# Loading x for the first read from a second copy laid out for it, in pieces of one chunk over 128 partitions with 8 KB rows

## The reference

```
xn = layernorm(x)                                  # over the 2048 channels
qkv_in = rat_read(xn)    # 4 channels of each of 512 groups -> 3 x 512, normalised, gamma and beta
q, k, v -> rope -> causal attention, 16 heads of 32 -> attn_out
h = rat_write(xn, attn_out); m = rat_read(h) -> gate, up (2048 wide) -> silu(gate) * up
h = rat_write(h, m)
x = x + tanh(g_xattn) * h
x = x + tanh(g_ffn) * (layernorm(x) @ sign) * softplus(scale)
```

## Time and profile before

| | |
|---|---|
| time of the kernel before, median of 3 runs | 2212.17 us (2210.51 to 2214.36) |
| profiled execution, its own time | 2214.25 us |
| its span in the profile | 2212.4 us |
| PE busy | 1981.1 us (90%) |
| DVE / ACT / POOL busy | 1415.1 / 978.9 / 423.3 us |
| moved by DMA | 453.87 MB, 205 GB/s on average |

### The profile page before, as it was taken

One profiled execution on the slowest core, in us unless ns is written; L12 is line 12 of the kernel. 1 busy time (PEld: TensorE's weight loads), 2 busy tenths in 40 slices (PEclk: granted clock), 3 DMA queues, 4 the chain that ended last, 5 costly groups with the idle time before them and its releaser, 6 DMA issues.

```text
span 2212.4 us, 25095 instructions
## 1 busy us (share of the span) xinstructions
PE 1981.1 (90%) x9562; PEld 1378.9 (62%) x9562; DVE 1415.1 (64%) x1563; ACT 978.9 (44%) x1376; POOL 423.3 (19%) x325
## 2 busy tenths in 40 slices
PE   2789897999999996289989999999999999989997
PEld 0344456666566553157767777777777677766786
DVE  3677767677777755958657638758639658468100
ACT  3656652787788875044145233143341162431100
POOL 1000004676555550000000001110001000011111
PEclk9899997999999997699999999999999999999999
DMA  8848346686666743246666657777658677559675
GB/s 198 186 110 187 91 102 207 238 289 235 239 239 223 265 171 128 100 165 235 230 238 225 248 186 218 233 243 261 227 191 234 207 263 277 224 162 258 156 183 136
DMA packets 180924, 453.87 MB, mean 205 GB/s; under 512 B 64320, under 2 KB 64576, under 8 KB 165440
## 3 DMA queue, kind: packets, MB, share of 16 engines
q1 hardware_dynamic: 146160, 313.31, 42.3%
q0 software_dynamic: 32480, 128.46, 20.9%
q10 hardware_dynamic: 2160, 10.43, 1.3%
HBM read 304.80 MB, written 147.32 MB: 204 GB/s over the span
## 4 chain that ended last, share of the span: by engine, by line
PE 44%; DVE 7%; DMA 5%; ACT 4%; issue 2%; SPq 0%; POOL 0%; DVEq 0%; POOLq 0%; ACTq 0%
PE ps L1788 16%; PE ps L1598 8%; PE ps L1600 7%; PE ps L1599 7%; DMA sign_h<-sign_h_scratch 2%; DMA up<-up_s_scratch 2%; PE ps L1657 1%; PE ps L1666 1%; PE ps L1695 1%; ACT L1817 1%; PE ps L1618 1%; DVE Y L2111 1%; PE ps L1707 1%; DVE DL_attn L2018 0%; DVE E_attn L2023 0%
## 5 line engine op out<-in xcount | busy, mean ns | idle before, releaser
L1788 PE MATMUL ps<-XH,sign_h 128*128 128x512 f32 x768 | 308.9, 402 | 13.5 <-DMA sign_h<-sign_h_scratch 8.7
L1788 PE MATMUL ps<-XL,sign_h 128*128 128x512 f32 x768 | 302.9, 394 | 0.0
L1159 DVE TENSOR_REDUCE maxes<-ps 128x1 f32<-128x512 f32 (+3 forms) x384 | 207.8, 554 | 97.4 <-PE ps L972 75.0
L1598 PE MATMUL ps<-ZH,up 128*128 128x512 f32 x512 | 205.3, 401 | 15.5 <-DVE ZL L2136 8.9
L1599 PE MATMUL ps<-ZL,up 128*128 128x512 f32 x512 | 201.0, 392 | 0.0
L1600 PE MATMUL ps<-ZH,up 128*128 128x512 f32 x512 | 200.9, 392 | 0.0
L1086 ACT ACTIVATE probs<-ps 128x512 f32<-128x512 f32 (+3 forms) x384 | 167.5, 485 | 50.6 <-PE ps L999 29.9
L1788 PEld LDWEIGHTS ps<-XH,sign_h 128*128 128x128 f32 x768 | 146.0, 190 | 60.9 <-issue 13.0
L969 PE MATMUL ps<-turned_k,turned_q 96*128 96x512 f32 (+3 forms) x384 | 157.6, 424 | 12.0 <-DVE maxes L1159 10.0
L1015 PE MATMUL ps<-probs,v_ones 128*64 128x512 f32 (+3 forms) x768 | 167.3, 514 | 0.3 <-ACT probs L1086 0.3
L1788 PEld LDWEIGHTS ps<-XL,sign_h 128*128 128x128 f32 x768 | 146.3, 191 | 31.6 <-issue 1.9
(11 more groups left out here) (334 smaller groups left out, 4169.4 us busy)
## 6 DMA issues: line engine op xcount, KB each, us to landing
sign_h<-sign_h_scratch SPq DMA_DIRECT2D x256, 256.0 KB, 3.8
up<-up_s_scratch SPq DMA_DIRECT2D x58, 1024.0 KB, 6.4
proj<-proj_s_scratch SPq DMA_DIRECT2D x58, 640.0 KB, 4.1
X<-in_x POOLq DMA_DIRECT2D x16, 1024.0 KB, 15.4
xn_scratch<-X SPq DMA_DIRECT2D x16, 1024.0 KB, 14.2
sign_raw<-in_sign SPq DMA_DIRECT2D x32, 512.0 KB, 7.9
sign_h_scratch<-sign_high SPq DMA_DIRECT2D x32, 512.0 KB, 4.0
sign_l_scratch<-sign_low SPq DMA_DIRECT2D x32, 512.0 KB, 5.3
```

Source lines behind the costliest of these rows:

```text
L1159: eng.tensor_reduce(MAXES[:, e, q, k0 // T:k0 // T + 1], ps[:, MX[m % 2], 0:w], AX.X, ALU.max).then_inc(mx_read.sem, mx_read.unit)
L1598: eng.matmul(out_ap, lh, rh, start=start, stop=False, skip_group_check=True)
L1788: mm = eng.matmul(ps[:, sign_bank(m)], s[q][:, f], x[:, n], start=n + w == 0, stop=n == NF - 1 and w == len(operands) - 1, skip_group_chec ...
```

## The change

The program gets a further input, `x_read`, which holds the same values as `x` in another order: [4 tiles, 4 chunks, 128 partitions, 2048], laid out before launch exactly as X wants it. A transfer now carries one chunk a of a tile for all 128 partitions: 128 rows of 8 KB, which stand one behind the other in HBM. There are again four transfers of 1 MB for a tile, C = HC = 4, so the waits' values stay as they are. The stores of xn keep `rows_of_x` and their four blocks of 32 partitions.

```diff
+def piece_of_x(t, x_read, a, n):
+
+    return (t["X"][:, n % 2, a * C:(a + 1) * C], x_read[n, a])
...
                 eng.wait_ge(loaded.sem, loaded.at(k=len(loads)))
-                for c in range(C):
-                    eng.dma_start(*rows_of_x(t, io["x_c"], c, 0)).then_inc(t["x_in"][0].sem, t["x_in"][0].unit)
+                for a in range(HC):
+                    eng.dma_start(*piece_of_x(t, io["x_read"], a, 0)).then_inc(t["x_in"][0].sem, t["x_in"][0].unit)
...
                 eng.wait_ge(w_in.sem, w_in.at(0, 4))
-                for c in range(C):
-                    eng.dma_start(*rows_of_x(t, io["x_c"], c, 1)).then_inc(x_in[1].sem, x_in[1].unit)
+                for a in range(HC):
+                    eng.dma_start(*piece_of_x(t, io["x_read"], a, 1)).then_inc(x_in[1].sem, x_in[1].unit)
                 for n in range(2, NB):
                     half = n % 2
                     eng.wait_ge(xn_out[half].sem, xn_out[half].at(n // 2 - 1, C))
                     eng.wait_ge(rd.sem, rd.at(n - 2, 3 * HC))
-                    for c in range(C):
-                        eng.dma_start(*rows_of_x(t, io["x_c"], c, n)).then_inc(x_in[half].sem, x_in[half].unit)
+                    for a in range(HC):
+                        eng.dma_start(*piece_of_x(t, io["x_read"], a, n)).then_inc(x_in[half].sem, x_in[half].unit)
...
+    io["x_read"] = args["x_read"].rearrange("n a p (j t) -> n a p j t", j=C)
...
         "x": x.reshape(B * L, HC, P, C).transpose(3, 1, 2, 0).reshape(NF, P, B * L),
+        "x_read": x.reshape(NB, T, HC, C, P // C, C).transpose(0, 2, 5, 4, 3, 1).reshape(NB, HC, P, C * T),
```

More of the change, by code:

```diff
@@ L2237, in build @@
     io["xn"] = xn.rearrange("f p t -> p f t")
-    for name, rows in (("x_c", args["x"]), ("xn_c", xn)):
-        io[name] = [rows[c * HC:(c + 1) * HC].rearrange("a (j h) t -> h (a j) t", j=C) for c in range(C)]
+    io["xn_c"] = [xn[c * HC:(c + 1) * HC].rearrange("a (j h) t -> h (a j) t", j=C) for c in range(C)]
+    io["x_read"] = args["x_read"].rearrange("n a p (j t) -> n a p j t", j=C)
     for name, shape in (("up_s", [NM, P, 2, 2 * HC * P]), ("proj_s", [NM, P, 2, WALL]), ("wall_s", [P, HC, 2, WALL]),
```

## The result

Over 15 timed executions the changed kernel takes 2202.37 us at the median, the kernel before 2218.05 us over 15. The ratio is 0.9935, 95% interval 0.9922 to 0.9948: 14.4 us faster, between 11.5 and 17.3 (the two medians lie 15.7 apart, inside that). The first three runs of the kernel before, 2212.17 at the median, were at the low end of its scatter (2210.5 to 2224.6). The profiled execution took 2199.85 us, its span is 2198.0 against 2212.4.

The account below looks back on a forecast made before the run. The prediction took PE's waits for two loads of X, tiles 0 and 3, as the bound; 11.6 + 4.0 = 15.6 us off the 2212.17 us median gave 2196.6 us, range 2191 to 2203.

Parts of the forecast that it names:

- from the median of 2212.17 it is 2196.6: Whole kernel: the summed gain of 15.6 us, taken off the median of the runs shown, gives 2196.6 us.
- the rest keeps its lengths: After the read phase: attention begins 15 to 16 us earlier and everything else takes as long as before.
- The first wait: Program start: the whole core waits for the load of tile 0; 11.6 us less, PE starting at about 17.4.
- 3.15 us are issue, first bytes and the last confirmation: Load of tile 0: fixed 3.15 us of the old 24.45, kept beside 9.75 us of transfer in the new load.
- The other route, x_last: Load of tile 0: four existing 1 MB, 128-partition loads on POOL's queue took 12.7 us, so tile 0 would take about that.
- The second wait: Tile 3 in the read phase: PE's 2.45 us stall and 1.5 us of lower-clock matmuls both go, 4.0 us together.
- The covered loads: Tiles 1 and 2 in the read phase: their loads are hidden before and after, so they gain nothing.
- rival 5: Block phase: the added input moves scratch tensors and slows up and sign weight streams; 2218.6 us at 25% growth, chance 0.03.
- rival 3: Tile loads: HBM or the queue gives only 326 GB/s, gain 8.4 + 4.0 us, time 2199.8 us; chance 0.05.
- The prediction's 88 us for those waits: Block phase: waits for up and sign weights, 2% + 2% of the span on the chain, put at some 88 us.
- The sum: Whole kernel: 11.6 us at the start plus 4.0 us at tile 3 make 15.6 us.

Follow-up runs that it names:

- the tile 0 kernel: Changed kernel with only tile 0 loaded in the new form, tiles 1 to 3 as before; ratio 0.9963 to the kernel before.
- the tile 3 kernel: Changed kernel with only tile 3 loaded in the new form, the others as before; ratio 1.0001 to the kernel before, 0.9970 when timed again.
- the kernel with the added input: Changed kernel with only tiles 1 and 2 loaded in the new form, the new 16.8 MB input present; ratio 1.0004 to the kernel before.

## Why the prediction came out as it did

**The step that failed** is the base of the sum, "from the median of 2212.17 it is 2196.6", and with it "the rest keeps its lengths". Both take the time of what the change does not touch as fixed, and three runs as enough to know it. The runs showed in its place 2218.05 us at the median of 15, and 2214.7 to 2218.4 in four further sets. They also showed an attention part of 499.6 or 505.1 us and a block part of 1356.0 or 1348.2 us in one and the same kernel. The base was 5.9 us too low, and the predicted time 5.8. The profiled execution of the kernel before, 2214.25 us, had the short attention part. That the three runs had it as well would explain the low base, but is not shown. Beside this, one term of the gain was mis-sized, as follows.

**The first wait.** Predicted 11.6 us, PE's start at 17.4. Measured 10.9 in the first profile; over all profiles of the two kernels the start is 28.88 on average before (28.99, 28.77) and 17.76 after (18.13, 17.69, 17.46), 11.1 us. The mechanism, the released barrier with all engines at once, is as described. The term that was mis-sized is "3.15 us are issue, first bytes and the last confirmation". It came from the old load, as the rest beyond 21.3 us at a full 197 GB/s, and had some 0.45 us of barrier in it (last landing at 28.5, release at 28.95). Taken from the new load, 13.1 to 13.6 us less 9.75, it is 3.4 to 3.8. The other route, x_last, gave 12.7 us from the first issue to the last landing. That is what tile 0 took too (12.6 to 13.0), but the 0.4 to 0.5 us from the landing to the barrier's release were left out of it, so the two routes agreed on two different things.

**The second wait.** Predicted 4.0 us, in two parts, the stall of 2.45 and 1.5 for matmuls at the lower clock (the 16 matmuls stand as 32 in the rows). Measured 4.01 between the closing matmul of tile 1 and DVE's Y, and the x_mean took 3.64 us, at a granted clock of 1.00. The stall and the slow matmuls came back with the tile 0 kernel (1.88 and 5.34 us) and went with the tile 3 kernel. In timed runs the term is near what they can resolve. The agreement to 0.01 us is of one pair of profiles; the read part's lengths put it at 4.1 us on average (328.2 against 324.1 us).

**The covered loads.** Tile 1 and tile 2: predicted nothing, measured 1.0004. The store of xn kept its 197 GB/s and still hid.

**The place in HBM** (rival 5) and **the cap** (rival 3): not seen. The block part of the kernel with the added input (1352.2 us) is inside what the kernel before shows by itself (1348.2 and 1356.0), and the matmuls' waits for sign and up weights overlap. The prediction's 88 us for those waits was the share of the DMA entries on the chain; the matmuls' own waits for them come to 16.0 us in the same profile.

**"The rest keeps its lengths".** Between executions of one kernel the attention part has two lengths some 6 us apart and the block part differs by up to 8 us (1348.2 and 1356.0 in the kernel before), so single profiles cannot show it, and the end of the first profile (14.4 us earlier) agrees with the read part's 14.4 by chance. The attention part began 14.4 us earlier in the first pair of profiles and 14.8 on average over three and two, not 15 to 16. Of the 0.56 us that were lost between the first matmul and the closing matmul of tile 1, 0.31 are in the first x_mean (5.54 against 5.23 us); the rest was not taken apart.

**The sum.** 15.6 predicted; 14.4 measured, interval 11.5 to 17.3, and in two further timings 0.9934 and 0.9932, 14.6 and 15.1 us. The forecast of the gain lies inside that interval. The absolute time was 5.8 us too low, 2196.6 against 2202.37, which lies 0.6 us inside the range's upper end. Taken off 2218.05, the same 15.6 us give 2202.45; that this meets the measured time to 0.1 us is luck, since the gain is known to 3 us. The rows' own differences could not have told the base; the spread of three runs, 2 us to either side, was taken for the kernel's, which is 7.

## What to carry to other kernels

Look at how many partitions a transfer touches before looking at its row length: with the engines' share at 1.0 and the rate at half, the transfer here sat on a quarter of the partitions, and a copy of the input in the tile's own layout removed that. Such a load is worth something only where an engine stands at it; two of the four were on the path, and the list of waits named both. If the first load of a program is what all engines wait for, issue it ahead of the wait for small constants, from a queue that did not hold the barrier (SP's here): that took PE's start to 15.6 and 16.4 us, with 0.9927 and 0.9926 to the kernel before, which is 1.5 us better than the change and not separable from it by these timings. And take the base of a forecast from more than three executions where the kernel's own scatter is half of the forecast gain.

## What I had not expected of the hardware

After the idle stretch of PE at the barrier ahead of the attention part PE's clock rises to 2.4 GHz to stay (0.99 on average to the end of the part in the first profile of either kernel) 38 to 42 us into the part in 7 of 18 profiles and 54 to 56 us into it in 11, nothing between, in both ways for one and the same kernel. (In three of the 18 it was up for some 3 us in between.) The part takes 498.9 to 500.1 us in the first form and 505.1 to 505.7 in the second. What decides it stayed open: it is not the kernel alone, nor the moment of PE's start alone, since starts of 28.60, 28.62 and 28.99 gave the short part and 28.77 and 29.08 the long one. One thing goes with it in these traces. Counted from the start of the part, the clock fell at 0.2 to 0.6 us in all 11 long ones; in the seven short ones it fell earlier in four, at 0.2 in one and at 2.1 to 2.3 in two. Whether that is the cause was not tested. 1 MB transfers to 32 partitions held 197 to 201 GB/s with both row lengths, the same as the stores from 32 partitions (197), with the DMA engines' share at 1.0, so the share alone does not tell a transfer at its best from one at half of it.
